# Perceiver layer on one core: three context batches loaded into another tensor's home, a new load order, the softmax's turning in two steps, and a new order of the steps

## What is computed

```
x = x + LayerNorm-cross-attention(x, ctx)      # ctx: 8 x 1601 x 256, linear attention: no softmax
x = x + local causal softmax attention(x)      # window 64, 16 heads of 16
x = x + FFN block(x): softmax attention with rope and compressed keys, RMSNorm,
        shared SwiGLU expert + 8 experts with a top-2 gate, RMSNorm
```

## Time and profile before

| what | value |
|---|---|
| runs | 235.42, 236.37, 236.45 us; median 236.37 |
| profiled execution's own time | 236.0 us |
| its span | 234.2 us |
| mean granted PE clock | 0.995 |
| PE busy | 222.3 us, 95% of the span |
| DVE, ACT, POOL busy | 172.9, 124.7, 75.8 us |

### The profile page before, as it was taken

One profiled execution on the slowest core, in us unless ns is written; L12 is line 12 of the kernel. 1 busy time (PEld: TensorE's weight loads), 2 busy tenths in 40 slices (PEclk: granted clock), 3 DMA queues, 4 the chain that ended last, 5 costly groups with the idle time before them and its releaser, 6 DMA issues.

```text
span 234.2 us, 5962 instructions
## 1 busy us (share of the span) xinstructions
PE 222.3 (95%) x2424; PEld 200.0 (85%) x2424; DVE 172.9 (74%) x372; ACT 124.7 (53%) x244; POOL 75.8 (32%) x101
## 2 busy tenths in 40 slices
PE   7999999999999998889999999999999999999992
PEld 6999898999999987778988999987778889998881
DVE  0759986886697699997975888978797774377344
ACT  3661961448356577656156798875653455740000
POOL 3012241030511616403526536594710032521010
PEclk9999999999999999999999999999999999999998
DMA  6799998996312612061301213033000000000001
GB/s 209 246 313 388 295 372 266 328 347 194 100 42 62 211 61 73 31 206 69 92 3 34 80 72 90 3 91 92 0 3 0 3 0 3 0 3 22 3 0 67
DMA packets 9435, 26.17 MB, mean 112 GB/s; under 512 B 1464, under 2 KB 2880, under 8 KB 9280
## 3 DMA queue, kind: packets, MB, share of 16 engines
q1 hardware_dynamic: 9120, 25.27, 32.7%
q10 hardware_dynamic: 288, 0.52, 0.7%
HBM read 25.27 MB, written 0.52 MB: 110 GB/s over the span
## 4 chain that ended last, share of the span: by engine, by line
PE 79%; DVE 8%; issue 5%; ACT 5%; DMA 2%; POOL 0%; POOLq 0%; DVEq 0%; ACTq 0%
PE ps L710 74%; PE ps L713 5%; DMA raw<-in_ctx 2%; ACT probT L518 1%; ACT ch L585 1%; DVE cl L1157 1%; DVE swapped L1261 1%; DVE Z L1146 1%; DVE straight L1265 1%; DVE straight L1262 1%; DVE mx L1235 1%; DVE prob L1245 1%; DVE swapped L1264 1%; ACT aT L518 1%; DVE sm L1243 0%
## 5 line engine op out<-in xcount | busy, mean ns | idle before, releaser
L710 PE MATMUL ps<-ch 128*128 128x130 f32 (+1 forms) x208 | 54.2, 275 | 1.1 <-DVE cl L1157 1.1
L710 PE MATMUL ps<-ch,cl 128*128 128x260 f32 (+1 forms) x208 | 53.4, 315 | 0.0
L710 PE MATMUL ps<-w,hT 128*128 128x512 f32 (+1 forms) x204 | 46.1, 382 | 0.0
L710 PEld LDWEIGHTS ps<-ch 128*128 128x128 f32 (+1 forms) x208 | 40.8, 196 | 2.3 <-ACT ch L585 1.2
L710 PEld LDWEIGHTS ps<-w,hT 128*128 128x128 f32 x204 | 36.3, 188 | 7.2 <-issue 0.2
L473 POOL TENSOR_TENSOR rstd<-ve,half_exp 128x1 f32<-128x1 f32 (+1 forms) x22 | 13.6, 619 | 87.9 <-DVE ve L1036 87.7
L710 PEld LDWEIGHTS ps<-ch,cl 128*128 128x128 f32 (+1 forms) x208 | 40.5, 195 | 0.3
L1157 DVE TENSOR_TENSOR cl<-raw,ch 128x1024 fp32r<-128x1024 f32 (+4 forms) x31 | 31.9, 1055 | 11.4 <-ACT ch L585 11.2
L585 ACT ACTIVATE ch<-raw 128x1024 fp32r<-128x1024 f32 (+4 forms) x31 | 27.5, 917 | 7.4 <-DMA raw<-in_ctx 6.1
L710 PE MATMUL ps<-xHL,dense 128*128 128x256 f32 x192 | 24.6, 285 | 0.0
L710 PEld LDWEIGHTS ps<-xHL,dense 128*128 128x128 f32 x192 | 23.5, 191 | 0.3
(11 more groups left out here) (161 smaller groups left out, 397.3 us busy)
## 6 DMA issues: line engine op xcount, KB each, us to landing
raw<-in_ctx SPq DMA_DIRECT2D x22, 512.0 KB, 4.4
raw<-in_w SPq DMA_DIRECT2D x8, 512.0 KB, 3.8
stage<-in_dense SPq DMA_DIRECT2D x4, 512.0 KB, 6.5
w<-in_w SPq DMA_DIRECT2D x4, 256.0 KB, 6.9
w<-in_w SPq DMA_DIRECT2D x1, 1024.0 KB, 9.4
mask<-in_mask SPq DMA_DIRECT2D x1, 800.5 KB, 7.2
raw<-in_ctx SPq DMA_DIRECT2D x8, 65.0 KB
raw<-in_ctx ACTq DMA_DIRECT2D x2, 256.0 KB, 5.4
```

The costliest lines, as they stand in the source:

```text
L710: return pe.matmul(o, l, r, start=start, stop=stop, skip_group_check=not check)
```

## The change

1. A new tile `ahead` (3 batches, 39 KB of each partition) is placed on the home of `dense`. Context batches 1 to 3 are loaded there, not into `raw`. Their loads wait for nothing, and batch 3 is loaded by one DMA and a tail. `raw` holds batch 0, then batches 4 to 7. POOL clears the tail rows of `ahead` with one more memset, of 3 x 256 columns, ahead of the one for `ch`. ACT's `piece` 0 waits until batch 3 has been split.
2. The loads of weights and constants stand behind other chunks, and some share a semaphore.
3. `turn_p` is two steps: `turn_half` turns the first four blocks and lets ACT copy them, `turn_p` the other four.
4. The list of steps is rewritten nearly everywhere.

```diff
+AHEAD = 3
-        ("split", 0), ("split", 1), ("split", 2), ("gram_rows", 0), ("gram", 0), ("split", 3), ("evac", 0),
+        ("gram_rows", 0), ("gram", 0), ("split", 0), ("gram_rows", 1), ("split", 1), ("split", 2), ("split", 3),
...
+    ahead, nxt = place("ahead", [P, AHEAD, CH_B * ROWS + 1, D], at=where["dense"])
+    assert nxt <= where["raw"]
...
+    def raw_batch(b):
+        return ahead[:, b - 1, :, :] if 1 <= b <= AHEAD else raw[:, :, :]
...
             beside = {
-                2: [(cst[:, :], d_const, "const_in")],
-                5: [(X[:, :, :], d_x, "x_in"), (w0[:, 2, :, :], d_w0[:, 2, :, :], "wv_in"), (cols[:, :], d_cols, "cols_in"),
-                    (rows[:, 3, :], d_rows[3, :].partition_broadcast(P), "row_in")],
...
+                3: [(cst[:, :], d_const, "const_in")],
+                5: [(w0[:, 2, :, :], d_w0[:, 2, :, :], "wv_in"), (cols[:, :], d_cols, "bias_in"),
+                    (rows[:, 3, :], d_rows[3, :].partition_broadcast(P), "bias_in"), (X[:, :, :], d_x, "x_in"),
...
             for n in range(CH_B * B):
                 b, c = divmod(n, CH_B)
-                if b:
-                    sp.wait_ge(sem("low_done"), splits(n - CH_B))
+                if b > AHEAD:
+                    sp.wait_ge(sem("low_done"), splits(c if b == AHEAD + 1 else n - CH_B))
...
+                elif b == AHEAD and c == 0:
+                    sp.dma_start(raw_batch(b)[:, 0:CH_B * ROWS, :], src).then_inc(sem("ahead_batch"), 16)
...
             pool.memset(raw[:, CH_B * ROWS, :], 0.0).then_inc(sem("no_rows"), 1)
+            pool.memset(ahead[:, :, CH_B * ROWS, :], 0.0).then_inc(sem("no_rows"), 1)
...
-                elif step == "turn_p":
+                elif step in ("turn_half", "turn_p"):
                     t, kind = i
-                    for j in range(2):
-                        act.wait_ge(own("p_turned", t), 2 * turn_of(t, kind) - 1 + j)
-                        copy(probT[:, t % 2, 4 * j:4 * j + 4, :],
-                             ps[:, tile_bank(t) + j, :].rearrange("p (c n) -> p c n", n=P), own("probT", t))
+                    j = 0 if step == "turn_half" else 1
+                    act.wait_ge(own("p_turned", t), 2 * turn_of(t, kind) - 1 + j)
...
                 elif step == "piece":
                     piece_landed(act, i)
+                    if i == 0:
+                        act.wait_ge(sem("low_done"), splits(CH_B * (AHEAD + 1) - 1))
```

More of the change, by code:

```diff
@@ L120, in second_half_steps @@
     return [
[3 rows of a table removed]
-        ("piece", 1), ("gram_rows", 17), ("values1", 1), ("score", (1, 0)), ("gram", 17), ("turn_z", (0, 1)),
-        ("score_product", (1, 0)), ("proj2_product", 0), ("evac", 5), ("cross3", 4), ("keys2", 0), ("shares", (1, 0)),
-        ("split", 20), ("cross4", 4), ("cross1", 5), ("exp", (1, 0)), ("gram_rows", 18), ("gram", 18),
-        ("keys_roped", 0), ("gram_rows", 19), ("piece", 2), ("gram", 19), ("values2", 0), ("turn_p", (1, 0)),
-        ("score_product", (0, 1)), ("piece", 3), ("values", (1, 0)), ("score", (0, 1)), ("project", (1, 0)),
@@ L129, in second_half_steps @@
-        ("norm2", 1), ("shares", (0, 1)), ("norm2_end", 1), ("exp", (0, 1)), ("cross2", 5), ("evac", 6),
-        ("gram_rows", 20), ("split", 21), ("gram", 20), ("cross2_half", 5), ("cross2_product", 5), ("split", 22),
-        ("turn_z", (1, 1)), ("split", 23), ("proj2_product", 1), ("turn_p", (0, 1)), ("keys2", 1), ("values", (0, 1)),
-        ("project", (0, 1)), ("values2", 1), ("rms1", 0), ("gram_rows", 21), ("square", 0), ("cross3", 5),
-        ("gram", 21), ("keys_roped", 1), ("rms1_end", 0), ("cross4", 5), ("turn_x", 0), ("cross1", 6), ("piece", 4),
@@ L163, in second_half_steps @@
-        ("last_square", 0), ("turn_x", 3), ("turn_x", 2), ("experts_half", (1, 3)), ("last_root", 0),
-        ("experts_product", (1, 3)), ("experts", (1, 2)),
+        ("xo_product", 1), ("norm1", 1), ("values", (0, 0)), ("gram", 15), ("project", (0, 0)), ("norm1_end", 1),
+        ("norm2", 0), ("norm2_end", 0), ("split", 17), ("split", 18), ("gram_rows", 16), ("gram", 16),
[3 rows of a table added]
+        ("shares", (1, 0)), ("values2", 0), ("evac", 5), ("gram_rows", 17), ("gram", 17), ("cross4", 4),
+        ("gram_rows", 18), ("gram", 18), ("split", 20), ("cross1", 5), ("keys_roped", 0), ("turn_half", (1, 0)),
@@ new lines, in second_half_steps @@
+        ("turn_p", (1, 0)), ("score_product", (0, 1)), ("piece", 3), ("values", (1, 0)), ("gram_rows", 19),
+        ("score", (0, 1)), ("project", (1, 0)), ("norm2", 1), ("gram", 19), ("shares", (0, 1)), ("norm2_end", 1),
+        ("exp", (0, 1)), ("split", 21), ("gram_rows", 20), ("gram", 20), ("split", 22), ("cross2", 5), ("evac", 6),
+        ("split", 23), ("cross2_half", 5), ("cross2_product", 5), ("turn_z", (1, 1)), ("turn_half", (0, 1)),
+        ("proj2_product", 1), ("turn_p", (0, 1)), ("keys2", 1), ("values", (0, 1)), ("cross3", 5),
@@ new lines, in second_half_steps @@
+        ("project", (0, 1)), ("rms1", 0), ("rms1_end", 0), ("values2", 1), ("square", 0), ("gram_rows", 21),
+        ("cross4", 5), ("gram", 21), ("keys_roped", 1), ("cross1", 6), ("turn_x", 0), ("exp", (1, 1)),
+        ("score_product", (1, 1)), ("gram_rows", 22), ("xo_product", 2), ("score", (1, 1)), ("xo", 2),
+        ("shares", (1, 1)), ("gram", 22), ("evac", 7), ("xo_end", 2), ("gram_rows", 23), ("gram", 23), ("cross2", 6),
[3 rows of a table added]
+        ("cross2", 7), ("proj1_product", 2), ("piece", 4), ("cross3", 7), ("queries", 2), ("piece", 5), ("turn_x", 1),
@@ L585, in _ @@
                         act.activation(halves(ch[:, c, lo:n, :])[:, :, :, 0:P],
[L586 removed]
+                                       halves(raw_rows(i, lo, n)), ACT.Copy).then_inc(sem("high_done"), 1)
                 elif step == "evac":
```

178 lines of the change are left out of this document (98 added, 80 removed), and 17 rows, old and new, of the table USES.

## The result

The changed kernel takes 232.57 us (median of 6 runs, 232.30 to 234.47) against 236.12 (median of 6, 235.42 to 236.45): ratio 0.9876, 95% interval 0.9855 to 0.9897 (the medians alone give 0.985; the reason is the two groups of times below). I had forecast 236.0 with a range of 233.7 to 238.1, so it is faster than the whole range.

The account below looks back on a forecast made before the run. PE was taken as the bound, busy 222.3 of 234.2 us. Profiled 236.0 - 2.9 + 0.75 + 0.6 + 1.1 + 0.1 = 235.65 us; the median, 0.37 above the profiled execution, was forecast at 236.0, range 233.7 to 238.1.

Parts of the forecast that it names:

- I give them nothing: New loads of context rows, weights and constants: claimed to gain 0, since PE hardly waits for `cl`.
- my own signs of being wrong: PE's busy time changes over 1 us, the first product moves, or PE's waits (10 to 229 us) leave 3 to 6.
- Waits that go: PE's waits for `aT`, `zT`, `prob`, `mb`, `cv`, Z and `xT` shrink or vanish: 2.9 us gained.
- The ceiling of 4.2 us: PE's short waits inside the program, before the last product, were put at 4.2 us in all.
- Waits that come: New PE waits where the new list takes away cover: 0.75, 0.6 and 1.1 us.
- place B: `turn_x` 0 and scores of tile 1: `mb` and `svn` delay Z; PE waits 0.6 us, bounds 0.2 and 1.2.
- Place A: Chunk 8, split behind a DVE chain of 5.83 us against PE's 5.08: PE waits 0.75 us, bounds 0 and 1.2.
- the five places at 1.1 us: `pre` 0, scores (0,1), `hidden_half` 0, `values` (2,0), `turn_z` (3,1): tighter, 0 to 2.5 us together, 1.1 taken.
- The end: `finish` 2 now directly ahead of `finish` 3, in DVE's wait for the last root: costs 0.1 us, bounds 0 and 0.4.
- The wait for `cl` behind chunk 4: PE's 0.2 us wait for chunk 4's split, which follows ACT's evacuation of batch 0's Gram matrix: should stay.
- ACT's wait for context rows: ACT's idle time before its splits should fall from 6.1 to about 3 us with no effect on PE.
- The crowded start: Rival, chance 0.05: SP's fuller queue takes bandwidth from chunks 0 and 1, PE starts later; 237.8 us.

Follow-up runs that it names:

- e5: The kernel before with 11 instead of 9 products on zeros ahead of the first Gram product; 235.69 us, 1.0006 against the kernel before.
- e7: e2 with context batch 3 loaded by three DMAs instead of one; 234.12 us, 0.9935 against the kernel before.
- e8: e7 with 11 instead of 9 products on zeros ahead of the first Gram product; 234.44 us, 0.9944 against the kernel before.
- e6: The changed kernel with 11 instead of 9 products on zeros ahead of the first Gram product; 232.54 us, 0.9869 against the kernel before.
- e9: e5 with the load of weights Wv moved from behind chunk 5 to behind chunk 2; 235.65 us, 0.9986 against the kernel before.
- e17: The changed kernel unaltered, run again; 232.64 us, 0.9868 against the kernel before.
- e2: The changed kernel with the old lists of steps, keeping the new loads and homes; 240.11 us, 1.0183 against the kernel before.
- e3: The kernel before with the new lists of steps and turning in two steps, keeping the old loads and homes; 241.51 us, 1.0230 against the kernel before.
- e11: e6 with `project` directly behind `values` again at (1,0) and (3,0); 233.28 us, 0.9900 against the kernel before.
- e16: e6 with SP again waiting for the split of chunk n-3 before requesting chunk n, for batch 1 alone; 235.00 us, 0.9968 against the kernel before.

## Why the prediction was wrong, step by step

The gain from 235.8 to 232.5 us splits in two: e5 to e7 or e8 (loads, old order) 1.3 to 1.6 us, and from there to e6 (order) 1.6 to 1.9 us. The two executions profiled first, both at the late pace (236.0 and 234.47), differ by 1.5 us, about the share of the order.

**The step that failed first: the loads, "I give them nothing".** The reasoning was that PE hardly waits for `cl`. That was true of the one execution I had, in which PE ran its first four microseconds of Gram products at the lower pace and so came to chunk 5 just when the chunk did. DVE's split of chunk 5 and PE's first product with it in the kernel before:

```profile
17.88 1.48 DVE L1157 TENSOR_TENSOR cl<-raw,ch 128x1280 fp32r<-128x1280 f32 x1
```

```profile
19.50 0.31 PE L710 MATMUL ps<-ch 128*128 128x130 f32 x1
```

The split ends at 19.36 and PE starts 0.14 us behind it, about the distance of e9 (18.91 and 19.06), where the list has a wait of 0.82 us for it; here it has none. With the early pace, which I did not know to exist, the kernel before runs into the held rows and gives the 1.7 us back (e5 and e9, both with 11 products; an early execution with 9 was not profiled), and the changed one keeps them (e17). The list of waits of one execution had no row for it. What the trace did show, and I read past, was ACT's idle 6.1 us for context rows: 1.4 of it before chunk 3 and 2.5 before chunk 6, on either side of the chunk for which PE had no slack. One of my own signs of being wrong came true with it: PE's waits between 10 and 229 us sum to 2.4 us, under the 3 that I had set. I also took order and loads as independent; e2 and e3 show that each needs the other.

**Waits that go: 2.9 forecast.** Too small. The three waits for `aT` went whole (1.4, I had 1.15), `zT` 0.6 (0.3), `prob` 0.5 (0.35), and also Z (L1052) 0.3, `xT` 0.3, `mb` 0.5, `z0T` 0.2 and half of `cv`: about 4.0 us by the lists. The ceiling of 4.2 us for waits inside the program was too low as well, since the list has three more rows (`kblk` 0.4, `kvcT` 0.4, `z0T` 0.2). At tile 3 a single `turn_z` stands between `values` and `project`, and I had given it its own 0.2 us; it takes a wait away on either side of itself, as e11 shows by bringing both back.

**Waits that come: 2.45 forecast.** Too large; 1.2 came: `gab` 0.5, which I had not listed, Z at place B 0.5, `kblk` 0.2 more.

Place A (0.75) is next to nothing. DVE at that place after the change:

```profile
33.02 0.87 DVE L1209 SCALAR_TENSOR_TENSOR cv<-rows,gpre,ps 128x256 f32<-128x256 f32 x2 [0.34 <-PE ps L742]
33.81 0.15 DVE L1172 TENSOR_SCALAR nan_a<-ps 128x4 f32<-128x4 f32 x1
34.01 0.16 DVE L1174 TENSOR_TENSOR nan_b<-nan_a 128x4 f32<-128x4 f32 x1
34.20 1.67 DVE L1177 SCALAR_TENSOR_TENSOR Z<-Z,nan_b,rows 128x256 f32<-128x256 f32 x4
35.91 0.42 DVE L1221 TENSOR_TENSOR mb<-ps,cst 128x256 f32<-128x256 f32 x1
36.26 0.34 DVE L1228 TENSOR_SCALAR svn<-ps,bvn 128x2 f32<-128x2 f32 x2
36.51 1.48 DVE L1188 TENSOR_TENSOR cl<-ahead,ch 128x1280 fp32r<-128x1280 f32 x1
```

and PE at its first product with chunk 8, with no wait that the list shows:

```profile
38.14 0.30 PE L742 MATMUL ps<-ch 128*128 128x130 f32 x1
```

From 33.02 to the end of the split at 37.99 it is 4.97 us, not 5.83: the masked rows take 2.10 us here. The 2.86 of the earlier trace rows were what they took there: `nan_b` 0.49 us against 0.16, and one of the four additions to Z 0.92 against 0.48. POOL adds rows to X from 31.73 to 33.85 us at that place, and in the changed kernel POOL does nothing there; whether that is the cause no run tested. So the duration of the same instructions elsewhere was the wrong price. PE's stretch from `flags` is 5.3 us, against my 5.08, and PE takes the chunk 0.15 us behind the end of its split, so the two arrive together: `cross4` 1 ahead of it lasts 0.50 us instead of 0.36 from start to start (32.72 to 33.08 us in the kernel before), a hidden wait of about 0.14 us. The bounds 0 to 1.2 held the value, the sum took the wrong one.

Place B (0.6) was right in size:

```profile
107.40 0.44 PE L745 MATMUL ps<-cst,Z 128*128 128x128 f32 x2 [0.51 <-DVE Z L1095]
```

0.51 us for Z, where I had 0.4 and some at the scores. Of the five places at 1.1 us, one shows anything (`hidden_half` 0, 0.2 us by starts of steps).

**What no term had.** Waits behind the first Gram product fell by 2.8 us by the lists, but the span by 1.7 between e7 and e6. The rest is in times that no row of the list has: where steps follow each other in another way, single steps take 0.2 to 0.3 us more from start to start (`values1` 1 0.67 to 0.95, the second product of batch 6 0.68 to 0.98). The modelled ends of matmuls can hide short waits, as at place A, so some of it may be waits after all; the runs don't separate the two. Here the lists of waits overstate what removing them brings.

The end (0.1): from PE's last product to the end of the span it is 4.7 us, 4.6 before. The wait for `cl` behind chunk 4 stayed, ACT's wait for context rows fell to 2.5 us (I had "about 3"), ACT's busy time fell from 124.7 to 120.2 us; all near the forecast (5.1 us of table loads). The crowded start didn't come: the first split starts at 5.04. ACT's fewer table loads were no visible part of the gain.

## What to carry to other kernels

Before a load is called hidden, ask how much earlier its user could come, and compare that with the transfer's own chain (request, landing, split): here the chain of chunk 5 was in balance with PE in the one execution profiled and was the bound in others. Test a change of loads and a change of order together and apart; either alone can lose what both gain. When a duration is carried from one place to another, look whether the same instructions take as long elsewhere. When a stop of PE costs more than its length, read the granted clock behind it: in e2 the lower level added 1.7 us, in four executions of e16 some 1.6. If the times of one kernel fall into two groups, profile both before explaining a difference.
